# Attention's value products, two key blocks together instead of one at a time

## The reference

```python
B, S, D, H = 8, 1024, 256, 16; KPH = 8
Q, K, V = ...                      # B x H x S x 8 each (of Q only the first 8 of 16 columns)
scores = jnp.einsum('bhsk,bhtk->bhst', Q[..., :KPH], K) / math.sqrt(KPH)
attn = jax.nn.softmax(scores, axis=-1)
ao = jnp.einsum('bhst,bhtv->bhsv', attn, V)
```

## Time and profile before

| | us |
|---|---|
| three runs, median | 4307.8 |
| three runs, lowest and highest | 4300.36, 4310.11 |
| the profiled execution | 4303.44 |
| its span, first to last instruction | 4301.7 |

### The profile page before, as it was taken

One profiled execution on the slowest core, in us unless ns is written; L12 is line 12 of the kernel. 1 busy time (PEld: TensorE's weight loads), 2 busy tenths in 40 slices (PEclk: granted clock), 3 DMA queues, 4 the chain that ended last, 5 costly groups with the idle time before them and its releaser, 6 DMA issues. The chain is left out here.

```text
span 4301.7 us, 64980 instructions
## 1 busy us (share of the span) xinstructions
PE 3569.5 (83%) x19727; PEld 2087.7 (49%) x19728; DVE 3346.4 (78%) x4247; ACT 2312.5 (54%) x4132; POOL 1348.1 (31%) x873
## 2 busy tenths in 40 slices
PE   8968888889449968877779999999999996569950
PEld 3445555555335557767723333333333333459950
DVE  8959999999764456665588989988898874758868
ACT  6855555554764432220028888888888883123323
POOL 4449888889003332220000000000000002744430
PEclk9989999999779979988869999999999996579985
DMA  6754444443767842228512222223232203422249
GB/s 212 254 202 167 162 166 163 161 167 123 266 204 179 195 119 68 68 68 226 162 41 54 68 58 64 67 55 71 51 72 52 70 8 101 135 70 91 90 150 294
DMA packets 534073, 536.92 MB, mean 125 GB/s; under 512 B 84720, under 2 KB 439792, under 8 KB 533664
## 3 DMA queue, kind: packets, MB, share of 16 engines
q1 hardware_dynamic: 507328, 475.20, 37.5%
q0 software_dynamic: 13952, 37.74, 2.6%
q10 hardware_dynamic: 12544, 20.98, 1.9%
HBM read 317.41 MB, written 215.19 MB: 124 GB/s over the span
## 5 line engine op out<-in xcount | busy, mean ns | idle before, releaser
L2131 DVE TENSOR_REDUCE at_top<-at_psM 128x1 f32<-128x1024 f32 x1024 | 1205.9, 1219 | 136.5 <-PE at_psM L1982 135.5
L2091 ACT ACTIVATE at_probs<-at_psS 128x512 f32<-128x512 f32 x2048 | 1060.9, 603 | 250.6 <-PE at_psS L2008 250.5
L2008 PE MATMUL at_psS<-at_q,at_k 64*128 64x512 f32 x2048 | 794.8, 468 | 8.3 <-ACT at_probs L2091 8.3
L575 POOL TENSOR_TENSOR sc_prod<-sc_state,sc_c_row 128x1024 f32<-128x1024 f32 x256 | 709.1, 2789 | 117.8 <-DVE sc_state L724 109.6
L1982 PE MATMUL at_psM<-at_k,at_q 62*128 62x512 f32 x2048 | 689.4, 451 | 36.3 <-DMA at_vraw<-scratch_vf 22.1
L724 DVE TENSOR_TENSOR_SCAN sc_state<-sc_dec,sc_psI 128x1024 f32<-128x1024 f32 x256 | 578.4, 2280 | 53.9 <-PE sc_psI L645 30.0
L1982 PEld LDWEIGHTS at_psM<-at_k,at_q 62*128 62x128 f32 x2048 | 312.8, 190 | 601.9 <-DVE at_top L2131 519.4
L2021 PE MATMUL at_psV<-at_probs,at_v 128*32 128x512 f32 x4096 | 546.3, 605 | 0.0
L656 PE MATMUL sc_psY<-sc_prod,sc_ident 128*128 128x512 f32 x1024 | 466.7, 596 | 3.5 <-DVE sc_y L710 2.2
L606 ACT ACTIVATE sc_dec<-sc_dt,sc_a_exp 128x1024 f32<-128x1024 f32 x256 | 293.6, 1148 | 311.3 <-DVE sc_state L724 308.5
L2008 PEld LDWEIGHTS at_psS<-at_q,at_k 64*128 64x128 f32 x2048 | 337.4, 184 | 195.8 <-ACT at_probs L2091 191.3
(11 more groups left out here) (394 smaller groups left out, 5068.9 us busy)
## 6 DMA issues: line engine op xcount, KB each, us to landing
sc_c_row<-scratch_bc SPq DMA_DIRECT2D x128, 512.0 KB, 4.1
scratch_xs<-at_zeros SPq DMA_DIRECT2D x140, 264.0 KB, 4.6
sc_b_row<-scratch_bc SPq DMA_DIRECT2D x64, 512.0 KB, 5.1
ec_y<-scratch_ys SPq DMA_DIRECT2D x32, 512.0 KB, 6.8
ex_x<-scratch_xs SPq DMA_DIRECT2D x39, 264.0 KB, 3.3
si_x<-in_x SPq DMA_DIRECT2D x16, 512.0 KB, 4.4
scratch_xn<-si_xn SPq DMA_DIRECT2D x16, 512.0 KB, 5.1
scratch_x_t<-si_xT SPq DMA_DIRECT2D x16, 512.0 KB, 5.7
```

Of the source, the lines that this page charges most:

```text
L575: pool.tensor_tensor(prod[:, (n * H + h) % 8, :], state[slot][:], c_row[n % ROWS][:], ALU.mult).then_inc(prod_ready, 1)
L2008: pe.matmul(psS[v % 3][:], rows_of(k4[j], h, 0, GROUP)[:, c * P:(c + 1) * P], rows_of(q4[j], h, 0, GROUP)[:, half * TILE:(half + 1) * TILE ...
L2091: act.activation(probs[:, slot(j, v), :], psS[v % 3][:], ACT.Exp).then_inc(act_done, 1)
L2131: dve.tensor_reduce(top[j % 2][:, h, c:c + 1], psM[t % 2][:], AX.X, ALU.max, negate=True).then_inc(maxed, 1)
```

## The change

The value products are issued after every fourth step instead of every second, and then two groups of them. At step 5 come the groups 0 and 1, at step 9 the groups 2 and 3, at step 33 the groups 14 and 15. TensorE's order, per eight scores, was 4 scores (with four maxima products), 1 group, 4 scores, 1 group; it becomes 8 scores (with eight maxima products), 2 groups. All instructions and all semaphore values stay.

```diff
@@ -2065,8 +2065,9 @@
                                 if at == 0:
                                     pe.wait_ge(top_in[nj], nb * 16 * QUAD + 16 * QUAD)
                                 step(u + 1, nj, nb, at, final and j == NQ - 2, final and j == NQ - 3)
-                            if s % 2:
-                                values(u, j, s // 2 - 1)
+                            if s % 4 == 1:
+                                for g in range(s // 2 - 2, s // 2):
+                                    values(u, j, g)
 
                 for b in range(B):
                     sequence(b, b == B - 1)
```

## The result

The changed kernel takes 4,444.5 us (median; 4,441.7 to 4,444.9), the kernel before 4,306.8 in the same comparison: ratio 1.0321, 95% interval 1.0308 to 1.0333. It is slower by 138 us; the forecast was 153.5.

What follows compares the result with a forecast made beforehand. Two almost equally late loops, scores through ScalarE and maxima through VectorE, set the 2.60 us period. Losses of 147.6 + 3.0 + 0.4 + 2.5 = 153.5 us on 4,307.8 gave 4,461 us, range 4,430 to 4,500.

Steps and rivals of the forecast that it cites:

- 2, fifth M behind the first reduction: New block: the fifth maxima product must wait for the first reduction to free its buffer, until +2.04 us.
- 3, seventh M behind the second: New block: the seventh maxima product waits for the second reduction until +3.18 us; the last pair starts at +3.51.
- Step 5: End of the new block's scores: value products start 0.42 us behind the last score product, at +3.93.
- Step 6: Two value groups in a row: four passes, 1.90 us until the next maxima product, block 5.83 us, +0.61.
- 0.47 per transposition: Once per unit (a batch element and four heads), the transposition sets the first reduction 0.47 us late, uncovered in the new block.
- TensorE as the bound: Rival: TensorE bounds the kernel and the change takes work off it; 44 us faster, 4,264; chance 0.05.
- Dearer in a row: Rival: two value groups together take 2.04 us or more, the third pass waiting for weights; 4,497 us; chance 0.07.
- Nothing changes: Rival: the products are hidden or TensorE starts maxima products while value products run; 4,308 us; chance 0.03.
- Milder loss: Rival: some wait in the new block overlaps better than added, 0.2 us per block; 4,410 us; chance 0.04.
- steps 1 to 3: New block: first reduction starts at +0.76 us; fifth and seventh maxima products wait for VectorE until +2.04 and +3.18.
- The clock falls: Rival: TensorE's two gaps of about 0.4 us per block lower its clock; block some 8.6 us, 5,100 in all; chance 0.02.
- step 4: ScalarE in the new block: the last score needs the fifth exponential, free at +3.23 us, under the 3.51 set by VectorE.

Runs made afterwards that it cites:

- the tiny ones: Kernel before and paired order, both with row maxima over 64 of 1024 scores and exponentials of 32 of each 512 columns: 4,100.4 and 4,033.6 us.
- the last experiment: Kernel before, with the second product of every second maxima tile made twice, to fill TensorE's gap before a period's last score: 1.0025 of before.

## Why the prediction was right, and where it was off

The mechanism held: VectorE can be at most two tiles behind TensorE, and the value products, joined into a longer piece, starved it. By the prediction's steps, measured from the block's first M in the rows above:

| step | predicted | measured |
|---|---|---|
| 2, fifth M behind the first reduction | +2.04 | +2.04 |
| 3, seventh M behind the second | +3.18 | +3.17 |
| 3, last pair | +3.51 | +3.50 |
| 5, value products | +3.93 | +3.83 |
| 6, next block | +5.83 | +5.69 |
| unit | 47.11 | 46.03 |

The unit is from a pair of equal rows of VectorE, one unit apart:

```profile
2686.98 4.62 DVE L2132 TENSOR_REDUCE at_top<-at_psM 128x1 f32<-128x1024 f32 x4 [1.10 <-PE at_psM L1982]
...
2733.01 4.62 DVE L2132 TENSOR_REDUCE at_top<-at_psM 128x1 f32<-128x1024 f32 x4 [1.09 <-PE at_psM L1982]
```

**Step 5 was mis-sized**: 0.42 us from the last S to V became 0.32. I took it from a last S that had waited for an exponential; in the new block the last S rides behind a pair and waits for nothing. The weight loads (PEld) tell the two apart. In the earlier trace rows the load of the waiting S starts together with its product (2710.30 and 2710.31) and the product takes 0.49; in the new block the last load starts 0.23 ahead of its product, which takes 0.39:

```profile
2706.60 0.19 PEld L2008 LDWEIGHTS at_psS<-at_q,at_k 64*128 64x128 f32 x1
```

That the 0.10 is this bare load is read from rows in both kernels and in the tiny ones (0.40 and 0.33); the last experiment only rules out the gap. I didn't change the load alone.

**Step 6 was mis-sized by 0.04**: V to next M 1.86, not 1.90, the middle passes being a little closer than the 0.45 I took. Together 0.14 us in a block, 8 x 0.14 x 30 = 34 us over the units, less 1 us of the transposition: 30 x 3.84 = 115 us instead of 147.6. The estimate of 0.47 per transposition held (46.03 - 8 x 5.69 = 0.51).

**A term too small made up for nearly half of it, and that was luck.** The last ten blocks and the half block with maxima ahead of them were to cost 2.9 us (2.5 and 0.4) and cost 14.7. The step that failed there was the clock: I had it as a rival for the whole stage at 0.02, and held against it that TensorE kept 1.00 at 82% busy without maxima. That was the old order. It didn't fall in the steady stretch (busy 87%, as predicted; clock 1.00), it did fall in the last unit, and for single bursts elsewhere: twice in the stage a pair of groups took 3.1 us instead of 1.9, after a transposition's block; VectorE then stands 2.5 us instead of 1.07, 2.8 us in all. The first of the two:

```profile
2324.51 4.62 DVE L2132 TENSOR_REDUCE at_top<-at_psM 128x1 f32<-128x1024 f32 x4 [2.50 <-PE at_psM L1982]
```

Without these 14.6 us of unforeseen clock the time would have been about 4,430, the lower end of the range.

The sum now: 115.2 + 5 x 0.47 + 14.7 + 2.8 = 135. The profiled spans differ by 141.5; 5.5 of the rest lie in other phases (3.0 ahead of the first reduction, 2.5 behind the last copy), which the edit doesn't touch. The medians differ by 138, as the profiled execution of before lay 3.4 under its median.

**The rivals.** TensorE as the bound: refuted for this kernel, its saving of 0.24 us per eight scores shown where little else holds TensorE. The 0.09 us that I read as the cost of going from S to V is not in the new block: V comes 0.32 behind the last S, and a pair of M and S costs 0.33. Here the rule of the Trainium skill (TensorEngine Tiling (Array Packing), Key Properties: a change of tiling mode drains the engine) agrees in direction, half as many changes being quicker; how much of the 0.24 is drain, how much the bare load of a waiting score and how much the waits that were left, the runs don't separate. *Dearer in a row*: refuted, a pair costs 1.86 against twice 0.99. *Nothing changes*: refuted by the ratio. *Milder loss*: none of steps 1 to 3 overlapped better. *The clock falls*: not in the steady stretch, but in the last unit and twice elsewhere; its price was also added up too low, since 3.4 us more in each of 256 blocks make about 5,170 and not 5,100.

**What the prediction had not said** is that the score loop alone would have made the change slower: with the reductions halved the pairing still costs 66 us, 55 of them ahead of the last stretch. It was in step 4 (+3.23 for the last S), hidden behind the larger wait.

## What to carry to other kernels

Joining one engine's work into longer pieces can save it a switch, and can cost an engine that lives from its other work a longer drought. With two buffers between them, compare the way from a freed buffer to the next tile behind the piece with two tiles of the consumer's time. Here that way was 0.06 + 0.33 + 0.32 + 1.86 + 0.76 = 3.33 us (release, pair, way to the value products, the piece, next tile) against 2.26, and the difference is the 1.07 that VectorE stood. When a duration is taken from a row to price a new order, see whether that row's instruction had waited: a product released by a semaphore took 0.49 us here, the same product further back in the queue 0.39. And look at the clock in the thinnest stretch of the stage, not only in the steady one.

## What the runs showed of the hardware

In the last unit the same products got another clock when they were only ordered otherwise. In the old order, with TensorE busy 84% of a window without maxima, the granted clock stayed at 1.00; in the paired order it went between its two levels within single blocks, 0.77 on average, and it was 1.00 again once the exponentials between were shortened. With four groups in a row it fell in the steady stretch too (0.75 to 0.87), where the whole loss was about twice what the starving alone had been reckoned at; how much of that the clock took was not measured apart.
